# A two-layer graph network with a routed feed-forward part: blocks worked one half later, four weighting matrices, group sums fetched in pairs

## The reference, cut to what matters

```python
def _gcn_layer(x, W, b, edge_weight, edge_src, edge_dst):
    support = x @ W
    msgs = support[edge_src] * edge_weight[:, None]
    agg = jax.ops.segment_sum(msgs, edge_dst, num_segments=N_NODES)
    return agg + b
h = jax.nn.elu(_gcn_layer(_layernorm(x), W1, b1, edge_weight, src, dst))
h = jax.nn.elu(_gcn_layer(h, W2, b2, edge_weight, src, dst))
x = x + h
H = jax.nn.gelu(_layernorm(x) @ W1 + b1, approximate=False)      # 256 -> 1024
probs = jax.nn.softmax(H @ Wg + bg)                              # 8 experts
# the output adds probs[e] * (H @ Wd[e] + bd[e]) of the likeliest expert e
```

## Time and profile before

| | us |
|---|---|
| three runs | 6077.28, 6102.87, 6113.61 |
| their median | 6102.87 |
| the profiled execution | 6099.5 |
| its span in the trace | 6097.3 |

### The profile page before, as it was taken

How to read it: one execution, slowest core, us unless ns; L and a number is a source line. 1 busy time by engine, 2 the same in 40 slices (tenths; PEclk the granted TensorE clock), 3 DMA queues, 4 the chain that set the end, 5 groups by cost and what they waited for, 6 DMA issues and landing times.

```text
span 6097.3 us, 84880 instructions
## 1 busy us (share of the span) xinstructions
PE 3583.8 (59%) x21458; PEld 3354.3 (55%) x21459; DVE 2004.9 (33%) x6596; ACT 1121.6 (18%) x1692; POOL 3248.6 (53%) x3403
## 2 busy tenths in 40 slices
PE   3555555554555455465555655665656655566999
PEld 2444454444444445455555655555655555555888
DVE  6222222222222222233333333333333333336333
ACT  3111111111111111122222222222222222221111
POOL 5565666665666666544545544544455555542444
PEclk6666666666666666687777777777777777778999
DMA  7333333333333333223333333333333333323554
GB/s 237 90 91 89 94 94 91 91 91 90 93 91 92 92 93 92 75 84 93 97 95 97 101 95 95 96 96 95 96 96 97 96 97 97 97 86 108 179 177 157
DMA packets 248227, 627.26 MB, mean 103 GB/s; under 512 B 63397, under 2 KB 110458, under 8 KB 247490
## 3 DMA queue, kind: packets, MB, share of 16 engines
q0 software_dynamic: 170688, 492.87, 27.9%
q1 hardware_dynamic: 76930, 129.30, 5.9%
HBM read 519.25 MB, written 103.63 MB: 102 GB/s over the span
## 4 chain that ended last, share of the span: by engine, by line
issue 27%; PE 26%; another core or an unknown queue 22%; DVE 11%; DVEq 9%; ACT 2%; ACTq 1%; DMA 1%; SPq 0%; POOL 0%; POOLq 0%
PE pA L1170 13%; PE pA L1292 6%; DVE S L853 4%; PE pB L1208 3%; DVEq L359 1%; DVEq L882 1%; DVE aggT L892 1%; PE pZ L1180 1%; DVEq L892 1%; DVEq L853 1%; DVEq L975 1%; PE pC L1282 1%; PE pB L1282 1%; DVEq L370 1%
## 5 line engine op out<-in xcount | busy, mean ns | idle before, releaser
L537 POOL DMA_INDIRECT rows<-h_scratch,idx x1568 | 1485.1, 947 | 1485.2 <-PE pA L1170 828.7
L1170 PE MATMUL pA<-S,rows 128*128 128x96 f32 x12544 | 1894.0, 324 | 521.6 <-DVE S L853 320.7
L1170 PEld LDWEIGHTS pA<-S,rows 128*128 128x128 f32 x12544 | 1852.9, 238 | 606.3 <-DVE S L853 436.3
L537 POOL DMA_INDIRECT rows<-xn_scratch,idx x1568 | 1488.4, 949 | 921.1 <-issue 425.2
L892 DVE TENSOR_TENSOR aggT<-aggT,pA 128x192 f32 x784 | 277.3, 354 | 3285.4 <-remote 1620.3
L630 ACT ACT_TABLE_LOAD x196 | 251.5, 1283 | 4204.3 <-DVE aggT L892 3002.3
L853 DVE TENSOR_SCALAR S<-iota_p,tdst,twgt 128x96 f32<-128x96 f32 x3152 | 863.9, 344 | 11.3 <-issue 7.5
L1180 PE MATMUL pZ<-wg,stage 128*128 128x256 f32 x784 | 310.8, 536 | 856.1 <-ACT stage L630 611.6
L1180 PEld LDWEIGHTS pZ<-wg,stage 128*128 128x128 f32 x784 | 186.4, 263 | 896.5 <-ACT stage L630 623.1
L1208 PE MATMUL pB<-work,w 128*128 128x128 f32 x3232 | 592.2, 362 | 75.3 <-issue 73.4
L1198 PE MATMUL pT<-ident,work 128*128 128x128 f32 x206 | 67.5, 429 | 941.6 <-DVE work L930 717.8
(11 more groups left out here) (173 smaller groups left out, 2282.6 us busy)
## 6 DMA issues: line engine op xcount, KB each, us to landing
pay_scratch<-work SPq DMA_DIRECT2D x98, 512.0 KB, 3.0
rows<-xn_scratch,idx POOLq DMA_INDIRECT x1568
rows<-h_scratch,idx POOLq DMA_INDIRECT x1568
h_scratch<-work SPq DMA_DIRECT2D x98, 128.0 KB
pay_scratch<-work SPq DMA_DIRECT2D x98, 128.0 KB
work<-in_x_dram SPq DMA_DIRECT2D x97, 128.0 KB
...
```

The lines of the kernel that those rows point to most:

```text
L537: pool.indirect_dma_start(rows[:, s, t, :], None, source, bass.IndirectOffsetOnAxis(at, 0))\
L1170: last = mm(to[:, k * W:(k + 1) * W], rows[:, slot, t, k * P:(k + 1) * P], Sx[:, t, :], start=(t == 0), stop=(t == T - 1))
```

## The change

Blocks are worked one half later than they are complete. The table in `regs` gets one row more (`NH + 1`), and each row's steps are those of the half before; `LEAD` becomes 3. DVE takes the step ahead of the half's four groups, PE behind them; ACT's staging copy waits for the additions of the half before. One more call of `ticks` stands behind each layer's loop. `S` has four places instead of two, and the matrices built after an addition are those for the group four later. A bank of `pA` holds two groups' sums (`group_sum`); PE waits once a pair for the bank, and DVE waits once a pair for both groups and then adds one, builds, adds the other, builds. The gate products of L1201 go to `pZ` instead of `pA`, behind a wait for `s_zb`, and the logits of a block are summed at the start of the next step (`logits_before`), for which PE's products into `pC` now wait (`s_lg`); before, that wait stood at the end of PE's step. The overflow path of PE waits for its additions. The source table is int16, and the highest target of a group is bounded on DVE from the lowest and the number of windows (by up to 95 nodes too high) instead of being fetched from PE.

```diff
-    LEAD = 2
+    LEAD = 3
...
-        tsrc = sb("tsrc", [P, T, TBL])
+        tsrc = sb("tsrc", [P, T, TBL], i16)
...
-        S = sb("S", [P, 2, T, W])
+        S = sb("S", [P, HALF, T, W])
...
-        pROW = (pC[0:1, 0:NG], pC[0:1, 512:512 + NG], pT[0:1, 0:NG])
+        pROW = (pC[0:1, 0:NG], pT[0:1, 0:NG])
...
-        pLG = pA[:, 1, KC * W:KC * W + NX]
+        pLG = pZ[:, C + KC * W:C + KC * W + NX]
+
+        def group_sum(u):
+            at = u % 2 * C
+            return pA[:, u // 2, at:at + KC * W]
...
             def stage_block(layer, j, h):
 
-                act.wait_ge(s_add[layer], HALF * (h + 1) + 2)
+                act.wait_ge(s_add[layer], HALF * h + HALF)
                 hold(act, s_z[layer], j + 1)
...
+                _, start, end = half_flags(act, NH)
+                ticks(act, start, end, lambda j: (tick1, tick2)[layer](j, NH))
...
-            tc.then(v.tensor_copy(HIr[:, 0:NG], pROW[1]))
-            tc.then(v.tensor_copy(NVf[:, 0:NG], pROW[2]))
+            tc.then(v.tensor_copy(NVf[:, 0:NG], pROW[1]))
+            tc.then(v.tensor_scalar(HIr[:, 0:NG], NVf[:, 0:NG], float(W), float(W - 1), ALU.mult, ALU.add))
+            tc.then(v.tensor_tensor(HIr[:, 0:NG], HIr[:, 0:NG], pROW[0], ALU.add))
+            tc.then(v.tensor_scalar(HIr[:, 0:NG], HIr[:, 0:NG], float(N - 1), None, ALU.min))
...
-            tc.then(v.tensor_tensor(FL, FL, A[:, 0:NH], ALU.add))
-            tc.then(v.scalar_tensor_tensor(out=FL[:, 1:NH], in0=A[:, 0:NH - 1], scalar=256.0, in1=FL[:, 1:NH],
-                                           op0=ALU.mult, op1=ALU.add))
-            tc.then(v.tensor_copy(regs[0:1, :, 0], FL))
+            tc.then(v.memset(FLX[:, NH:NH + 1], 0.0))
+            tc.then(v.tensor_tensor(FLX[:, 1:NH + 1], FLX[:, 1:NH + 1], A[:, 0:NH], ALU.add))
+            tc.then(v.scalar_tensor_tensor(out=FLX[:, 2:NH + 1], in0=A[:, 0:NH - 1], scalar=256.0,
+                                           in1=FLX[:, 2:NH + 1], op0=ALU.mult, op1=ALU.add))
+            tc.then(v.tensor_copy(regs[0:1, :, 0], FLX))
...
             def build_S(layer, g, half):
 
-                dve.wait_ge(s_mm[layer], g + (SLOTS - 1))
+                dve.wait_ge(s_mm[layer], g + (SLOTS - HALF + 1))
...
             def edges_half(layer, h, with_overflow):
 
-                for u in range(HALF):
+                for u in range(0, HALF, 2):
                     g = HALF * h + u
-                    if u % 2 == 0:
-                        pair = dve.value_load(regs[0:1, bass.ds(h, 1), 1 + u // 2], min_val=0,
-                                              max_val=(1 << 2 * PACK) - 1)
-                        bases = [nc.s_assert_within(one, 0, N - 1, skip_runtime_bounds_check_because=
-                                                    "a dst is below the number of nodes")
-                                 for one in (pair & ((1 << PACK) - 1), pair >> PACK)]
-                    hold(dve, s_add[layer], g + 2)
+                    pair = dve.value_load(regs[0:1, bass.ds(h, 1), 1 + u // 2], min_val=0,
+                                          max_val=(1 << 2 * PACK) - 1)
+                    bases = [nc.s_assert_within(one, 0, N - 1, skip_runtime_bounds_check_because=
+                                                "a dst is below the number of nodes")
+                             for one in (pair & ((1 << PACK) - 1), pair >> PACK)]
                     if with_overflow:
-                        overflow(layer, g, bases[u % 2])
-                    dve.wait_ge(s_mm[layer], g + 1 + SLOTS)
-                    to = aggT[:, :, bass.ds(bases[u % 2], W)]
-                    v.tensor_tensor(to, to, pA[:, u % 2, 0:KC * W].rearrange("p (k n) -> p k n", k=KC), ALU.add)\
-                     .then_inc(s_add[layer], 1)
-                    build_S(layer, g + 2, u % 2)
+                        hold(dve, s_add[layer], g + HALF)
+                        for n in range(2):
+                            overflow(layer, g + n, bases[n])
+                    dve.wait_ge(s_mm[layer], g + 2 + SLOTS)
+                    for n in range(2):
+                        hold(dve, s_add[layer], g + n + HALF)
+                        to = aggT[:, :, bass.ds(bases[n], W)]
+                        v.tensor_tensor(to, to, group_sum(u + n).rearrange("p (k n) -> p k n", k=KC), ALU.add)\
+                         .then_inc(s_add[layer], 1)
+                        build_S(layer, g + n + HALF, u + n)
 
             def z_biased(layer, j):
 
@@ -914,15 +925,25 @@
             def tick1(j):
                 z_biased(0, j)
                 elu(0, j, hout).then_inc(s_elu[0], 1)
...
-                if flows(0, j):
-                    dve.wait_ge(s_blkclear, j + 1)
...
+            def logits_before(j):
+
+                dve.wait_ge(s_payc, j + 1)
+                dve.wait_ge(s_log, j + 1)
+                v.tensor_reduce(lgpart[:, 0, :], pF[:, :, :, P:PG].rearrange("p b c e -> p e b c"),
+                                axis=AX.XY, op=ALU.add)
+                v.tensor_tensor(lgpart[:, 1, :], pLG, brow[:, 2 * C:2 * C + NX], ALU.add).then_inc(s_lgp, 1)
+                dve.wait_ge(s_lgp, j + 1)
+                v.tensor_tensor(LG[:, bass.ds(j * -1 + (NB + DEPTH), 1), :].rearrange("p b e -> p (b e)"), lgpart[:, 0, :],
+                                lgpart[:, 1, :], ALU.add).then_inc(s_lg, 1)
 
             def tick2(j):
                 bc.base, bc.n = 3 * j, 0
                 if flows(1, j):
                     z_biased(1, j)
+                logits_before(j)
...
-                dve.wait_ge(s_payc, j + 2)
-                hold(dve, s_log, j + 2)
-                v.tensor_reduce(lgpart[:, 0, :], pF[:, :, :, P:PG].rearrange("p b c e -> p e b c"),
...
+                    tc.then(v.memset(pC[:, :], 0.0))
+                dve.sem_inc(s_add[layer], HALF)
+                for u in range(HALF):
+                    build_S(layer, u, u)
                 with dve.Fori(0, ITERS) as i:
                     for half in range(2):
                         h = 2 * i + half
                         ovf, start, end = half_flags(dve, h)
+                        ticks(dve, start, end, (tick1, tick2)[layer])
                         with dve.If(ovf > 0):
                             edges_half(layer, h, True)
                         with dve.Else():
                             edges_half(layer, h, False)
 
                         stage_idx(layer, h + AHEAD, (i & 1) * 2 + half)
-                        ticks(dve, start, end, (tick1, tick2)[layer])
+                _, start, end = half_flags(dve, NH)
+                ticks(dve, start, end, (tick1, tick2)[layer])
                 if layer == 0:
                     tick1(NB)
             for j in range(NB, NB + DEPTH):
                 tick2(j)
+            logits_before(NB + DEPTH)
...
+                pe.wait_ge(s_lg, j + 2)
...
+                    pe.wait_ge(s_zb[1], j + 2)
                 for m in range(FUSED, KH):
                     last = mm(pLG, HT[:, m, :], identg[:, m, P:PG], start=(m == FUSED), stop=(m == KH - 1))
...
-                pe.wait_ge(s_lg, j + 2)
...
+                            pe.wait_ge(s_ovadd[layer], we)
                     pe.wait_ge(s_S[layer], g + 1)
-                    pe.wait_ge(s_add[layer], g + 1)
-                    products(s, S[:, s % 2, :, :], pA[:, s % 2, :], s_mm[layer])
+                    if u % 2 == 0:
+                        pe.wait_ge(s_add[layer], g + 2)
+                    products(s, S[:, u, :, :], group_sum(u), s_mm[layer])
...
+                _, start, end = half_flags(pe, NH)
+                ticks(pe, start, end, (tick1, tick2)[layer])
```

25 lines of the change are left out of this document (9 added, 16 removed).

## The result

The changed kernel takes 5735.33 us (median of 4 runs, 5730.26 to 5759.6); the kernel before stands at 6091.88 (4 runs, 6077.28 to 6113.61). The ratio is 0.942, 95% interval 0.9377 to 0.9462. It is faster, as forecast, but by 357 us and not by 680: the forecast was 5420 us, its range 4900 to 5650.

The account below looks back on a forecast made before the run. Bound: waits between engines, paced by POOL's gathers and their stops. Sum: 6099.5 - 84 (first layer) - 616 (second layer) + 15 + 4 (uncovered last block steps) + 3 (small steps) = 5421, say 5420 us; range 4900 to 5650.

Parts of the forecast that it names:

- The first layer: First edge layer: 23.65 us a half from POOL's gathers, 2318 us against 2402, 84 us less.
- The second layer: Second edge layer: 23.65 us a half instead of 29.9, 2318 us against 2934, 616 us less.
- its block products, 9.6 us: PE, second-layer half: block products follow the four groups, 19 to 21 us with waiting, inside a full stretch of gathers.
- PE's semaphore updates get through late: Both layers: PE's reports arrive late while POOL issues without a stop, some 10 us after the last group's matmuls.
- the second rival: Second layer: ACT's copy and PE's transposes stay on the path, near 27.5 us a half, 5880 us; chance 0.12.
- The stops: POOL, both layers: one stretch of 16 gathers and one stop a half, the stop costing about 3.5 us over 20.0.
- the slower rival: Both layers: two stops a half, 34.7 us in the second layer and 27.15 in the first, 6840 us; chance 0.04.
- The block's round trip: Second layer: PE's transposes to ACT's copy and back stay on the path, 27.5 us a half, 5880 us; chance 0.12.
- Gathers slowed by DVE: Both layers: DVE's denser runs lengthen each gather by 0.30 us, 28.4 us a half, 6352 us; chance 0.01.
- Early logits: Block step's start: logits summed ahead of PE's products, covered by PE's four groups, cost nothing; one more set 0.6 us.
- Pairs and four matrices: DVE's additions: waiting for both groups adds 1.8 us, hidden by four matrices; without that cover 706 us.
- PE's clock in the second layer: Sign in the profile after: PE clock in the second layer higher than the 0.77 of before.

Follow-up runs that it names:

- `paced`: Changed kernel with a 128 x 16 memset on POOL behind each gather and a wait for it; 6991.67 us, ratio 1.1446 to the kernel before.
- `thin_gathers`: Changed kernel with only the first of each group's four gathers issued; 3592.49 us, one run.
- `old_order`: Changed kernel with LEAD 2, table unshifted, block step behind the additions; four matrices, pairs and early logits kept; 6860.56 us, ratio 1.1262 to the kernel before.
- `after_again`: Changed kernel run again, on a chip where the kernel before took 4717.15 and 4725.29 us; 4673.94 us, ratio 0.9898.
- the clean kernel: Kernel before with only four matrices, pairs and two sums a bank, block steps unmoved; 4672.3, 4677.55 and 4670.77 us, ratios 0.9909, 0.9911, 0.9909.

## Why the prediction was right and wrong

**The first layer: the time right, its shape in part.** 23.65 us were taken from stretches of 16 gathers of the same loop, and 23.66 measured. But only 50 of the 126 stretches between stops have 16 gathers, and 44 have 12; there are 125 stops, 1.28 a half, each 2.77 us longer than the usual 1.25, where one a half of some 3.6 was forecast. The sum came out all the same, since a stop is the shorter the fewer gathers went before it: 12.04 us for 8 and 23.58 for 16, 17.89 for 12 (1015.66 to 1033.55 in the changed kernel), each time 1.47 to 1.51 us a gather. A price for each gather would have been the better reading. PE was held in this layer too, 7.7 us a half (753.9 us), and with 12.9 us of its own work (1090.03 of 2000 us) it still had time left.

**The second layer: wrong, and with it the number.** The step that failed is that PE works its groups "and then has its block products, 9.6 us", all of it in 19 to 21 us "inside a full stretch", and the 23.65 us taken from it "in both layers". The term was 2318 us for 98 halves and measured 2656. In place of PE's 17.9 us with some waiting there were 18.75 us of work and 8.3 us in which PE was held. The reading under it was half of the matter. "PE's semaphore updates get through late" held and is seen again (ACT's L666 waits 1558.9 us for one, DVE's L903 907.7). What I did not see is that PE's instructions themselves are held once enough of them fall into a stretch. Before, only the short groups and few others did, and the block products ran mostly while POOL was stopped, with an issue time of 73.4 us in 71 waits that was there to be read (L1208 above). A price for PE's long work beside gathers was in no row, and I took it from PE's busy time beside a stopped POOL. `paced` and `thin_gathers` show that the hold goes with the gathers, on the same chip. Both issue them less densely in time, so they do not tell POOL's issuing from what the transfers do behind it; only the bytes are ruled out. The rows for 23.65 came from a layer with some 68 matmul records a half and went to one with 121 (5759 in 2000 us of 23.66 us a half, 9359 in 2100 us of 27.1).

**The range.** The prediction named 29.9 us a half, today's second layer, as a bound of this term, but the range did not reach to it: its upper end of 5650 allows the second layer 2.3 us a half over 23.65. Half of the way from 23.65 to 29.9 is 26.8, and the second rival with 27.5 lay outside too, at 5880 us and a chance of 0.12.

**The stops.** One was forecast; the second layer has 1.85 on average. It was the pattern of the slower rival, at a small part of its price, since the block step of 11 us was covered all the same.

**The rivals.** The block's round trip was given 27.5 us a half, close to 27.1, and is the wrong mechanism: the products that need ACT's copy, L1210, sat idle 25.5 us in all in the changed kernel, the transposes L1238 not at all, and `thin_gathers` keeps the trip at 15.1 us a half. Gathers slowed by DVE: their mean in the second layer went from 947 to 956 ns, nothing like the 0.30 us of that rival. The Trainium skill's "SBUF — State Buffer", section "SBUF: two separate sides", says that GpSimd cannot write descriptors while VectorE holds the shared ports in a two-port mode. Taken to hold for DVE's matrices, it would have made the gathers longer, and the trace does not agree; no run here shows in which mode the matrices ran.

**Small terms.** Early logits at nothing, right (7.4 us of waiting), and `old_order` shows what stands without the cover. Pairs and four matrices at nothing in themselves: on the prompt chips they are worth 1%, not a loss. PE's clock in the second layer was to rise; it stayed at 0.77 on the late chip and was 0.87 on the prompt one (window 2300 to 4000 of `after_again`), where PE no longer stalls.

**Open.** Why some chips hold PE and others do not: the runs show that it goes with the chip and not with the kernel, and nothing of the cause. How much of the 5.8% on a late chip belongs to the delay and how much to the four matrices: `old_order` was confounded by the logits, and the clean kernel fell on prompt chips three times. What holds PE: the holds are measured, what makes them is not. The waits that vanished, ACT's staging before L1180 and DVE's copy before L1198 (PE idle 11.93 us in the earlier trace rows), are those that the delay takes away, but that is an argument and not a run.
